# Taking the next expert number out of its word in three places of a skill step

## What is computed

```python
rw = softmax(cond_8, axis=-1)                       # 32 x 8
w, sel = top_k(rw, 2)                               # which experts, 2 per item
w = w / w.sum(axis=-1, keepdims=True)
# gated MLP of one expert: gelu(x @ gate) * (x @ up) @ down, 128 -> 512 -> 128
out = sum over the 2 chosen experts of w * mlp(x[b], skill weights of that expert)
out = out + mlp(x, shared weights)
return x + out
```

## Time and profile before

| | before |
|---|---|
| median of 3 runs | 226.04 us (225.59 to 226.26) |
| the profiled execution, own time | 226.19 us |
| its span in the trace | 224.40 us |
| PE matmul busy share of the span | 95% |
| PE weight load busy share | 75% |
| DVE, ACT, POOL busy shares | 56%, 61%, 50% |
| skill steps | from about 82.5 us to the end |

### The profile page before, as it was taken

The page is one execution under the profiler, slowest core; times in us unless marked ns, Lnnn a source line. Parts: engine busy times, 40 slices in busy tenths (PEclk is TensorE's granted clock), DMA queues, the critical chain, the costliest instruction groups (busy, mean ns, idle before and its releaser), DMA issues.

```text
span 224.4 us, 7185 instructions
## 1 busy us (share of the span) xinstructions
PE 214.0 (95%) x2739; PEld 167.7 (75%) x2740; DVE 124.9 (56%) x224; ACT 136.3 (61%) x221; POOL 112.4 (50%) x113
## 2 busy tenths in 40 slices
PE   7884998999999999999999999999999999999995
PEld 3441454545444458899999999999999999999995
DVE  4594899486879997553443444434434434334341
ACT  5256775757887978665565564565554655655550
POOL 3042445444554566755545546456455465465552
PEclk9998899999999999999999999999999999999999
DMA  6999400000000000000010010010010010010011
GB/s 201 395 435 421 187 1 0 3 0 1 0 3 0 0 1 3 3 3 1 3 50 3 3 50 3 3 50 3 1 50 3 3 50 3 4 50 3 0 50 50
DMA packets 2671, 11.73 MB, mean 52 GB/s; under 512 B 336, under 2 KB 592, under 8 KB 2128
## 3 DMA queue, kind: packets, MB, share of 16 engines
q1 hardware_dynamic: 2496, 11.01, 12.3%
q10 hardware_dynamic: 144, 0.26, 0.5%
HBM read 9.18 MB, written 2.10 MB: 50 GB/s over the span
## 4 chain that ended last, share of the span: by engine, by line
PE 89%; DVE 1%; issue 0%; DVEq 0%
PE g_ps L565 9%; PE o_ps L583 7%; PE u_ps L565 7%; PE o_ps L585 6%; PE g_ps L567 6%; PE u_ps L567 6%; PE o_ps L584 6%; PE u_ps L566 6%; PE g_ps L566 6%; PE o_ps L546 3%; PE o_ps L548 3%; PE o_ps L547 3%; PE g_ps L533 3%; PE u_ps L535 3%; PE u_ps L533 3%; PE g_ps L535 3%
## 5 line engine op out<-in xcount | busy, mean ns | idle before, releaser
L242 POOL TENSOR_TENSOR h<-h 128x512 f16<-128x512 f32 x96 | 110.7, 1159 | 107.0 <-ACT h L274 69.9
L398 DVE SCALAR_TENSOR_TENSOR h<-gel,sk_factor,u_ps 128x512 f32<-128x512 f32 x64 | 47.8, 747 | 75.0 <-ACT gel L269 72.3
L269 ACT ACTIVATE gel<-g_ps,sk_gate 128x512 f32<-128x512 f32 x64 | 44.0, 687 | 56.6 <-PE g_ps L567 56.6
L274 ACT CAST h<-h 128x512 f16<-128x512 f32 x96 | 58.5, 609 | 1.7 <-DVE h L398 1.7
L565 PE MATMUL g_ps<-x,wsk 128*128 128x128 f16 x256 | 46.6, 221 | 0.4
L565 PE MATMUL u_ps<-x,wsk 128*128 128x128 f16 x256 | 46.3, 219 | 0.0
L567 PE MATMUL u_ps<-x,wsk 128*128 128x128 f16 x256 | 46.2, 219 | 0.0
L566 PE MATMUL g_ps<-x,wsk 128*128 128x128 f16 x256 | 46.2, 219 | 0.0
L566 PE MATMUL u_ps<-x,wsk 128*128 128x128 f16 x256 | 46.2, 219 | 0.0
L567 PE MATMUL g_ps<-x,wsk 128*128 128x128 f16 x256 | 46.2, 219 | 0.0
L585 PE MATMUL o_ps<-h,wsk 128*128 128x128 f16 x256 | 45.9, 219 | 0.0
(11 more groups left out here) (96 smaller groups left out, 307.6 us busy)
## 6 DMA issues: line engine op xcount, KB each, us to landing
wsk<-skills SPq DMA_DIRECT2D x3, 2048.0 KB, 17.2
outT<-xT SPq DMA_DIRECT2D x7, 256.0 KB, 2.0
xT<-xT SPq DMA_DIRECT2D x1, 1024.0 KB, 8.5
wsh<-shared SPq DMA_DIRECT2D x3, 256.0 KB, 3.7
xT<-xT SPq DMA_DIRECT2D x1, 768.0 KB, 6.5
xT<-xT ACTq DMA_DIRECT2D x1, 256.0 KB, 3.3
outT<-xT SPq DMA_DIRECT2D x1, 192.0 KB, 2.4
outT<-xT SPq DMA_DIRECT2D x1, 64.0 KB, 1.6
```

What stands on the lines that cost most here:

```text
L242: nc.gpsimd.tensor_tensor(hidden_lo(t), hidden_full(t), hidden_hi(t), ALU.subtract).then_inc(lo_ok, 1)
L269: nc.scalar.activation(gel[:, t % NG, :], g_ps[t % 2][:, :], ACT.Gelu_apprx_tanh, scale=scale).then_inc(gelu_ok, 1)
L274: nc.scalar.copy(hidden_hi(t), hidden_full(t)).then_inc(hi_ok, 1)
L398: nc.vector.scalar_tensor_tensor(out=h32[:, t % N32, :], in0=gel[:, t % NG, :], scalar=factor, in1=u_ps[t % 2][:, :], op0=ALU.mult, op1=AL ...
```

## The change

The expression for the expert number is no longer left whole until an address needs it. For step t + 1 the shift is worked out in step t ahead of the gate group, the mask ahead of the up group and the multiplication by 512 ahead of the down group; `pe.lower_val` puts the operation at that place. `gate_up_skill` becomes `half_skill`, called once for gate and once for up, and the result is kept in the table `e512`, which the down group six steps later uses as well. The matmuls, their order, their addresses and all waits stay.

```diff
-            def gate_up_skill(t, e512):
+            def half_skill(t, kind, e512):
...
+            def shifted(t):
                 n, m = divmod(t - SH, PER_WORD)
-                return ((word[n] >> (3 * m)) & (E - 1)) * I
-
+                s = word[n] >> (3 * m)
+                pe.lower_val(s)
+                return s
+
+            def masked(s):
+                e = s & (E - 1)
+                pe.lower_val(e)
+                return e
+
+            def columns(e):
+                a = e * I
+                pe.lower_val(a)
+                return a
+
+            e512 = {SH: columns(masked(shifted(SH)))}
             for t in range(SH, STEPS):
...
-                gate_up_skill(t, expert(t))
+                more = t + 1 < STEPS
+                if more:
+                    ahead = shifted(t + 1)
+                half_skill(t, GATE, e512[t])
+                if more:
+                    ahead = masked(ahead)
+                half_skill(t, UP, e512[t])
+                if more:
+                    e512[t + 1] = columns(ahead)
                 if t - LAG < SH:
                     down_shared(t - LAG)
...
-                    down_skill(t - LAG, expert(t - LAG))
+                    down_skill(t - LAG, e512[t - LAG])
             for t in range(STEPS - LAG, STEPS):
-                down_skill(t, expert(t))
+                down_skill(t, e512[t])
```

More of the change, by code:

```diff
@@ L553, in weights @@
                 return wsk[:, bass.ds(e512 + ((2 * kind + part) * E * I + c * P), P)]
-            def gate_up_skill(t, e512):
+            def half_skill(t, kind, e512):
                 b = (t - SH) // TOP_K
                 xh, xl = x2[:, b, 0, :], x2[:, b, 1, :]
[L558 to L568, removed]
+                w_hi, w_lo = ([weights(e512, kind, part, c) for c in range(C)] for part in range(2))
+                for ap in w_hi + w_lo:
+                    pe.lower_ap(ap, for_matmul_weights=True)
+                pe.wait_ge(gelu_ok if kind == GATE else h_ok, t - 1)
+                for c in range(C):
+                    cols = (g_ps, u_ps)[kind][t % 2][:, c * S:(c + 1) * S]
+                    nc.tensor.matmul(cols, w_hi[c], xh, start=True, stop=False)
+                    nc.tensor.matmul(cols, w_hi[c], xl, start=False, stop=False)
+                    last = nc.tensor.matmul(cols, w_lo[c], xh, start=False, stop=True)
+                last.then_inc((g_ready, u_ready)[kind], 1)
             def down_skill(t, e512):
@@ L642, in _ @@
                 skip_runtime_bounds_check_because="eight numbers of 0 to E - 1, three bits each")
-            def expert(t):
+            def shifted(t):
                 n, m = divmod(t - SH, PER_WORD)
-                return ((word[n] >> (3 * m)) & (E - 1)) * I
+                s = word[n] >> (3 * m)
[10 more added lines that the diff above has]
+            e512 = {SH: columns(masked(shifted(SH)))}
             for t in range(SH, STEPS):
```

## The result

The changed kernel takes 227.94 us (median of 6 runs, 226.13 to 228.25) against 225.94 us of the kernel before (6 runs, 225.59 to 226.26): a ratio of 1.0082, 95% interval 1.0051 to 1.0114. It is slower by about 2.0 us. The forecast was 226.7, range 224.0 to 227.6: slower was the likelier side (0.43), but the size lies above the range.

The account below looks back on a forecast made before the run. The prediction took PE's instruction stream, its time adding up over each step, as the bound. Moved words, waits and end counted 0, added words +0.7 us: median 226.04 became 226.7 us, range 224.0 to 227.6.

Parts of the forecast that it names:

- What bounds the kernel: Skill steps: PE's instruction stream takes longer than its 36 matmuls need; 6.1 us idle before first loads, 5.4 at gate.
- rate reading: Skill steps: the stream's time for all words, waits and matmuls adds up, so spreading words can't help; chance 0.75.
- burst: Rival at gate: each group's words must fit under the group before, so spreading helps; 223.9 us, chance 0.13.
- lead of 0.06 us: Before a gate group: the stream was ahead by 0.06 us after an on-time down group, and gate lost that much less.
- The words moved: Ahead of gate, up and down: 6, 4, 4 words become 4, 5, 5; at 0.10 us per lone word, moving costs 0.
- The words added: Skill steps with m = 0: seven of eight added lone words cost 0.10 us each, 0.7 us.
- The waits and the end: Wait words ahead of down and the last six down groups: no longer waits, end unchanged, 0.
- The dearer word: Rival: a lone word costs up to 0.138 us at its new place; up to 230.7 us, chance 0.06.
- The cheaper word: Rival: a lone word costs 0.085 us at its new place, partly covered by matmuls; 225.1 us, chance 0.06.
- What it said would show: Profile after: step 2.13 to 2.16 us, idle sum 6 to 7 us, some 3 us each at up and down.
- The reserve of the first skill steps: Early skill steps: PE's queue, full from the shared steps, lets groups start without gaps until near 102 us.
- The range: Whole kernel: 224.0 to 227.6 us, most of the rate reading, part of burst, the beginning of the dearer word.

Follow-up runs that it names:

- after_again: The changed kernel as it stands, run once more against the kernel before: 228.07 us, ratio 1.0088.
- one_more_up: The kernel before with one lone register word more, a second mask, ahead of up in each skill step: 231.76 us, ratio 1.0264.
- mask_up: Against the kernel before, shift and mask both moved ahead of up one step early, shift still lone, multiplication left at gate: 225.99 us, ratio 0.9998.
- packed_shift: The kernel before with mask ahead of shift, so the shift gets packed; no word moved or added: 227.57 us, ratio 1.0076.
- few: The kernel before with skill weights addressed through a view in bytes, two packed words a group instead of four: 219.38 us, ratio 0.9698.

## Why the prediction was wrong

*What bounds the kernel*: right, though not all of the stream's time lies in the words (last section). The rate reading held in every run that parts it from burst. Burst, at 0.13, is excluded by `after_again` (228.07, not 223.9) and `one_more_up` (231.76, not 227.1); that `mask_up` won nothing would fit both, but its idle time at down would not fit burst. One reading on the way was off: the six words of the earlier trace rows did not begin before the down load at 110.43. Their start, 110.4 in the row, is 110.44 in the trace, 0.01 us after the load. In the earlier trace rows it is 0.07 us after (144.64 against 144.57), so the lead of 0.06 us stands, and the conclusion with it.

*The words moved*: this is the step that failed. The prediction took 0.10 us for a lone word at any place, "the same instruction in the same stream", and from that "moving costs 0". For the mask and for the addition pushed out behind down that was right: in after a late gate group, with the mask and four packed words behind it, took 0.69 us to the first load of up, as said (the two rows below), the addition takes 0.097 us, and `mask_up`, which moves shift and mask as lone words, is at 225.99. It failed for the shift, which is not moved as a lone word. The order showed it going into a free place of a packed word (L648), and the text says so of that place; but it was never priced there. No row of before shows a packed word with a shift, so that was an operation to be bounded, and it was taken for free without a bound. The program divides there, and the word takes 98 to 106 ns instead of 74. By after's median of 28 ns more that is 1.6 us over 56 steps; `packed_shift`, where it is 24 ns, is 1.6 us slower by the medians (227.57) and 1.14 us slower in the 53 steps.

```profile
118.31 0.10 PEld L564 LDWEIGHTS g_ps<-x,wsk 128*128 x1
...
119.00 0.10 PEld L564 LDWEIGHTS u_ps<-x,wsk 128*128 x1
```

*The words added*: right in mechanism and near in size. 0.7 us was the term; after is 0.5 us over `packed_shift` (228.07 against 227.57), which has the packed shift without the added words. In the 53 steps the two profiles of the change are 0.58 and 0.81 us over that of `packed_shift`, and six of the added words lie there; about 0.1 us of that is the longer division (28 against 24 ns).

*The waits and the end*: nothing shows against them. From step 10 to 63 the only wait of PE's loads that the profiles name is "issue", 2.6 us before and 2.3 us after; no wait of PE for another engine appears there in either.

*The rivals.* The dearer word had the right sign and a wrong cause: it asked for more at the new place, and up to the 0.138 of a packed word; `mask_up` and `one_more_up` give 0.10 at up as at gate. The cheaper word is out as well. That the time moved to the likelier side is partly luck: the sum had 0.7 of the 2.0 us, and the larger part came from a term that it did not have.

*What it said would show.* The step was to be 2.13 to 2.16 us and is 2.166. The idle times were to sum to 6 to 7 us, and sum to 7.3; they were to share about evenly between up and down and stand at 1.8 and 4.8. The waits of every second step lie at down: in after the first down load comes 0.24 us after the last up load in the steps with a wait word, and 0.13 in the others. The reserve of the first skill steps was to last until near 102 us: it ended at 98.86 in a run that began them 1.86 us earlier, which is a step sooner than in the earlier trace rows.

*The range.* It reached 0.9 us above the forecast, to the beginning of one rival. Had the packed shift been bounded as the lone words were, between 0 and the 36 ns of a lone shift on top of the packed word, 56 x 0.036 = 2.0 us would have stood at the upper end, and 228 inside.

## What to carry to other kernels

Before spreading a burst of register work, settle whether the stream's time adds up over the loop: groups with the same burst that start without a gap while a queue is full, and a lead that is kept from a short burst to a long one, say that only fewer or cheaper instructions help, and a gap that is chased from one place comes up at the next. Read what the compiler makes of a moved operation, not only where it lands: an operation that gets into a packed instruction for free in the count can be another operation there. And when the engine's own stream is the bound, look at how addresses are formed; a view with a unit of one byte halved the packed words here and was worth 6.6 us.

## What the runs showed of the hardware beyond that

A packed word's time depends on what is in it: in `few` 42 ns with two operations, 51 with three and 74 with six; in before 74 with six additions and multiplications; in after 98 to 106 where one of the six is a division (L648 above), least with the largest divisor (98 in every step with m = 7).

What a word takes of the stream is more than its own duration. In the trace, from its start to that of the next word, a packed word of 74 ns takes 0.133 us, a lone one of 36 ns 0.101, and the word with a division 0.161 to 0.169 (medians from step 10 to 63 of before and after), each some 0.06 us over its duration. So a lone word of 36 ns costs 0.10 us, and the 24 to 32 ns of a division come through in full. The price of a lone word was the same by three other ways: 0.10 from one gate group with it and one without, 5.33 us for 53 of them in `one_more_up`, and 0.69 us for five words after a late group in after, as in the earlier trace rows.

One part of the rate account lies elsewhere than the prediction had it. By such medians (0.192 us where a group's 12 matmuls are issued between two words, 0.297 with a wait word as well) the stream of before needs 106.9 us for the 53 steps, about what PE needs (106.5 in `few`), and not the 113.1 measured. The other 6.2 us are words that start later than the median, by up to 0.16 us, almost always one in 58 instructions of the stream (a matmul and its weight load counted as two). In `mask_up`, `packed_shift`, after and `one_more_up` they add up to 6.0 to 6.6 us. So what these changes add is in the words, and what lifts the stream over PE is in these pauses; what causes them no run here shows.
